# Stacking K's rows for two batches at once, with the weight check's squares moved between score groups

## The reference

```
q = layernorm(x) @ Wq.T + bq;  k = ctx @ Wk.T + bk;  v = ctx @ Wv.T + bv
scores = q k^T / sqrt(16) / temperature[head];  attn = softmax(scores)
x = x + (attn v) @ Wo.T + bo
gate = layernorm(x) @ Wg.T;  up = layernorm(x) @ Wu.T      # integer weights x 1/127, 768 wide
x = x + (silu(gate) * up) @ Wd.T                            # Wd likewise
```

## Time and profile before

| | |
|---|---|
| time, median of 3 runs | 410.93 us (410.18 to 411.25) |
| the profiled execution | 409.33 us, span 407.6 us |
| mean granted TensorE clock | 0.975 of full speed |
| busy: PE / DVE / ACT / Pool | 363.9 / 298.2 / 256.2 / 158.7 us |
| all DMA traffic | 37.68 MB, mean 92 GB/s |
| Q rows: DMAs, size, median from issue to landing | 96, 128.0 KB, 4.5 us |
| K rows: the same | 96, 60.0 KB, 2.6 us |

### The profile page before, as it was taken

How to read it: one execution, slowest core, us unless ns; L and a number is a source line. 1 busy time by engine, 2 the same in 40 slices (tenths; PEclk the granted TensorE clock), 3 DMA queues, 4 the chain that set the end, 5 groups by cost and what they waited for, 6 DMA issues and landing times.

```text
span 407.6 us, 9738 instructions
## 1 busy us (share of the span) xinstructions
PE 363.9 (89%) x3398; PEld 326.9 (80%) x3398; DVE 298.2 (73%) x734; ACT 256.2 (63%) x564; POOL 158.7 (39%) x282
## 2 busy tenths in 40 slices
PE   0567578799999999999999999999998999998984
PEld 0566465688999899989999898999997988787984
DVE  6974657678878877787788778888777686745743
ACT  2353366577776767676777686767766675756442
POOL 3133313264434443343426263626353061613322
PEclk9979689999999999999999999999999999999989
DMA  6999595536523753184525591739137622010000
GB/s 174 294 101 155 76 157 88 87 76 123 101 65 77 141 118 78 33 161 110 112 58 89 124 157 32 141 53 159 26 84 83 113 31 81 15 42 2 27 27 27
DMA packets 61749, 37.68 MB, mean 92 GB/s; under 512 B 34049, under 2 KB 61185, under 8 KB 61697
## 3 DMA queue, kind: packets, MB, share of 16 engines
q1 hardware_dynamic: 61696, 36.99, 47.4%
...
## 4 chain that ended last, share of the span: by engine, by line
PE 67%; DMA 11%; SPq 6%; DVE 5%; ACT 4%; issue 3%; POOL 3%; ACTq 0%; DVEq 0%
PE ps_w L807 28%; DMA qs<-q 9%; PE ps_w L800 9%; PE ps_o L936 6%; PE ps_b L920 6%; PE ps_a L910 6%; SPq L395 5%; PE ps_w L792 5%; PE ps_w L819 4%; PE ps_w L840 3%; DMA ks<-k 1%; ACT probs L545 1%; DVE ks L695 1%; POOL hidT L463 1%; DMA probs<-wkT 1%
## 5 line engine op out<-in xcount | busy, mean ns | idle before, releaser
L463 POOL TENSOR_TENSOR hidT<-hid,hidT 128x256 fp32r<-128x256 f32 x80 | 58.9, 738 | 124.7 <-ACT hidT L538 124.7
L807 PE MATMUL ps_w<-xn2T,wg 128*128 128x256 f32 x384 | 103.0, 301 | 0.2 <-DVE xn2T L632 0.2
L807 PE MATMUL ps_w<-xn2T,wu 128*128 128x256 f32 x384 | 96.2, 282 | 0.0
L545 ACT ACTIVATE probs<-ps_b 120x512 f32<-120x512 f32 x128 | 76.0, 593 | 22.8 <-PE ps_b L920 22.5
L710 DVE TENSOR_REDUCE negmax<-ps_a 128x4 f32<-128x480 f32 x128 | 82.8, 648 | 8.7 <-PE ps_a L910 8.4
L807 PEld LDWEIGHTS ps_w<-xn2T,wg 128*128 128x128 f32 x384 | 72.9, 190 | 1.5 <-issue 0.5
L807 PEld LDWEIGHTS ps_w<-xn2T,wu 128*128 128x128 f32 x384 | 73.1, 190 | 0.0
L910 PE MATMUL ps_a<-ks,qs 96*128 96x120 bf16 x512 | 49.9, 222 | 12.0 <-DMA qs<-q 7.5
L556 ACT ACTIVATE tanh_g<-ps_w 128x256 f32<-128x256 f32 x96 | 36.8, 383 | 37.2 <-PE ps_w L807 35.9
L807 PE MATMUL ps_w<-wd,hidT 128*128 128x256 f32 x384 | 55.8, 293 | 3.0 <-POOL hidT L463 2.6
L920 PE MATMUL ps_b<-qs,ks 98*120 98x256 bf16 x256 | 50.6, 279 | 4.6 <-ACT probs L545 3.2
...
## 6 DMA issues: line engine op xcount, KB each, us to landing
qs<-q SPq DMA_DIRECT2D x96, 128.0 KB, 4.5
ks<-k SPq DMA_DIRECT2D x96, 60.0 KB, 2.6
...
```

Of the source, the lines that this page charges most:

```text
L463: nc.gpsimd.tensor_tensor(hidT[:, 1, f], hid[:, f % 2], hidT[:, 0, f].bitcast(F32), ALU.subtract).then_inc(hid_lo, 1)
L545: nc.scalar.activation(probs[0:NKV, e % PROBS], ps_b[0:NKV], ACT.Exp).then_inc(exp_done, 1)
L807: last = nc.tensor.matmul(dst, lhsT, rhs, start=(start and k == 0), stop=(stop and k == len(terms) - 1), skip_group_check=True)
```

## The change

1. `ks` becomes two buffers, each for a pair of batches side by side ([98, 16 heads, 2, 120]) in place of three for one batch. In even batches the six K DMAs carry both batches; in odd ones none is issued. A and B read their half. The counts of the semaphore `ks_in` follow pairs (`pair_count`).
2. The ones rows are set by two memsets on Pool, at its start, in place of three on DVE.
3. K's hi part waits for one pair instead of for two batches.
4. The six pieces of squares go from steps -20 to -9 to steps -10 to 12, between A groups of batch 0; tell, sum, told and read go later as well.
5. Nearly all entries of the tables that are for the first four and last three batches, and some lags (k third, q third, rsqrt1, ctx hi, k mid, hid lo, y, store, load x_res), take other values.

The tables, `SHIFT` cut to the kinds that the text speaks of, and the code:

```diff
 LAG = {
-    "load ctx": -90, "load x": -90, "ctx lo": -77, "rsqrt1": -75, "ctx hi": -70, "stats1": -70, "var1": -66,
-    "norm1": -55, "k hi": -52, "normT1 hi": -51, "k rest": -50, "normT1 lo": -49, "k rows": -46, "k mid": -43,
-    "q hi": -40, "q rows": -37, "k third": -37, "q rest": -37, "v": -35, "q mid": -33, "q third": -31,
-    "A": -16, "max": -13, "load x_res": 6, "shift rows": 14, "shift hi": 16, "shift lo": 19, "exp": 27,
+    "load ctx": -90, "load x": -90, "ctx lo": -77, "stats1": -70, "rsqrt1": -69, "ctx hi": -69, "var1": -66,
+    "norm1": -55, "k hi": -52, "normT1 hi": -51, "k rest": -50, "normT1 lo": -49, "k rows": -46, "k mid": -44,
+    "q hi": -40, "q rows": -37, "q rest": -37, "v": -35, "k third": -33, "q third": -33, "q mid": -33,
+    "A": -16, "max": -13, "load x_res": 7, "shift rows": 14, "shift hi": 16, "shift lo": 19, "exp": 27,
     "B": 27, "bias x_res": 30, "pv": 40, "pv copy": 43, "rsum": 63, "att": 64, "attT hi": 69,
     "attT lo": 70, "rsqrt2": 77, "x1": 78, "stats2": 79, "var2": 80, "norm2": 89, "normT2 hi": 89,
-    "normT2 lo": 91, "tanh": 94, "gate": 95, "hid": 96, "hid hi": 98, "hid lo": 100, "hid lo last": 118,
-    "y": 123, "store": 148,
+    "normT2 lo": 91, "tanh": 94, "gate": 95, "hid": 96, "hid hi": 98, "hid lo": 99, "hid lo last": 118,
+    "y": 122, "store": 146,
 }
 EVERY = {
     "rsum": 1, "k rows": 4, "q rows": 2, "exp": 4, "A": 4, "B": 4, "max": 4, "pv": 16, "pv copy": 15,
-    "tanh": 4, "gate": 4, "hid": 4, "hid hi": 4, "hid lo": 2, "y": 4,
+    "tanh": 4, "gate": 4, "hid": 4, "hid hi": 4, "hid lo": 2, "y": 5,
 }
 
 
 START = {
-    "load wv": -96, "load wo": -44, "load bv": -116, "load bo": -21, "weight q": -72, "weight o": -25,
-    "weight v": -51, "ones rows": -133, "load wg": (-57, -51), "load wu": (-47, -45), "load wd": (-42, -40), "int hi": (-46, -29, -21),
-    "int lo": (-36, -25, -18), "squares": (-20, -19, -15, -14, -11, -9), "tell": -3, "sum": 2, "told": 7, "read": 63,
+    "load wv": -96, "load wo": -47, "load bv": -124, "load bo": 10, "weight q": -74, "weight o": -35,
+    "weight v": -54, "load wg": (-57, -51), "load wu": (-51, -45), "load wd": (-42, -40), "int hi": (-46, -29, -22), "int lo": (-36, -25, -18),
+    "squares": (-10, -6, -2, 2, 6, 12), "tell": 14, "sum": 20, "told": 18, "read": 78,
 }
 
 
 SHIFT = {
-    "A": {0: 5, 1: 2, 3: -1, 14: -1, 15: -1},
+    "A": {0: 3, 1: 1, 2: -1, 3: -1, 13: -1, 15: -1},
+    "B": {1: -4},
...
-    "bias x_res": {0: -16, 1: 9, 2: 4, 3: -16, 13: 10, 14: 8, 15: -5},
-    "ctx lo": {0: -66, 1: -29, 2: -6, 3: 7, 14: -4, 15: -8},
-    "k hi": {0: -20, 1: 19, 2: 2, 15: -6},
-    "k rest": {0: -21, 1: -27, 2: -12, 3: -27, 13: 4, 15: -1},
-    "k rows": {0: 4, 1: -9, 15: 3},
-    "k third": {1: 6, 2: 4, 3: 4, 14: 3, 15: -4},
-    "load x": {0: -49, 2: -19, 3: -23, 13: -5, 14: -27, 15: -12},
-    "load x_res": {0: -1, 3: -1, 14: 22, 15: -9},
-    "max": {0: 1, 2: -1, 14: -2, 15: -2},
-    "q rows": {0: -3, 1: 5, 2: 6, 3: 5, 14: 1, 15: -1},
-    "q third": {2: 3, 3: 1, 15: 4},
-    "rsqrt1": {0: -71, 3: -3, 14: -6, 15: -3},
+    "bias x_res": {0: -17, 1: 23, 2: 4, 3: -16, 14: 6, 15: -9},
+    "ctx lo": {0: -22, 1: -27, 2: -5, 3: -14, 13: 6, 14: -6, 15: 8},
+    "k hi": {0: -23, 1: 14, 2: 3, 3: -2, 15: -14},
+    "k rest": {0: -19, 1: -35, 2: -12, 13: 4, 15: -2},
+    "k rows": {0: 4, 13: -20, 14: -2, 15: 5},
+    "k third": {0: 3, 1: 12, 2: -12, 3: 12, 13: -5},
+    "load x": {0: -12, 1: -4, 2: -1, 13: -6, 14: -18, 15: 7},
+    "load x_res": {0: 4, 2: -1, 3: -14, 13: -4, 14: -1, 15: -1},
+    "max": {0: -1, 2: -1, 13: -2, 15: -2},
+    "q rows": {0: -3, 1: 9, 2: 6, 3: 5, 13: 5, 14: 2, 15: -7},
+    "q third": {0: -1, 1: 3, 2: 5, 3: -5, 13: -3, 14: 4, 15: -5},
+    "rsqrt1": {0: -75, 1: -9, 2: 2, 3: -3, 13: -3, 14: -9, 15: -2},
-    "stats1": {0: -88, 1: -48, 2: -8, 3: -10, 13: -2, 14: -2, 15: -1},
+    "stats1": {0: -75, 1: -55, 2: -2, 3: -6, 13: -4, 14: -2, 15: -1},
-    "var1": {0: -73, 1: -11, 2: -5, 3: -9, 13: -3, 14: 1, 15: 1},
+    "var1": {0: -74, 1: -9, 2: -2, 3: -10, 14: -6},
...
+
+
+def pair_count(pair):
+
+    return (pair // 2 + 1) * (6 * 16)
 
 
@@ -253,7 +260,7 @@
 
 
         qs = [sb(f"qs{r}", [KS_ROWS + 2, H, NQ], BF16) for r in range(RING)]
-        ks = [sb(f"ks{r}", [KS_ROWS + 2, H, NKV], BF16) for r in range(RING)]
+        ks = [sb(f"ks{r}", [KS_ROWS + 2, H, 2, NKV], BF16) for r in range(2)]
         v_one = [sb(f"v_one{r}", [NKV, H, VW]) for r in range(RING)]
         negmax = sb("negmax", [P, RING, QT, H])
         shiftT = sb("shiftT", [H, 2, NQ], BF16)
@@ -286,7 +293,7 @@
         xres_in = [sem(f"xres_in{r}") for r in range(RING)]
         ctx_in = [sem(f"ctx_in{r}") for r in range(2)]
         qs_in = [sem(f"qs_in{r}") for r in range(RING)]
-        ks_in = [sem(f"ks_in{r}") for r in range(RING)]
+        ks_in = [sem(f"ks_in{r}") for r in range(2)]
         shift_in = [sem(f"shift_in{r}") for r in range(RING)]
         stored = [sem(f"stored{r}") for r in range(RING)]
 
@@ -385,14 +392,17 @@
             sp.dma_start(bq_col[:], bq).then_inc(temp_in, 16)
             load_weight("q", wqT)
 
-            def stack(kind, n, part, t, dst, arrived, parts):
+            def stack(kind, n, part):
 
                 at_least(sp, b_full, count(n - RING, GROUPS, GROUPS))
                 sp.wait_ge((hi, mid, lowest)[part][kind], job_count(kind, 0, n))
-                src = t[:, part, :, n % 2] if kind == "k" else t[:, part]
+                if kind == "k":
+                    dst, src, arrived, parts = ks[n // 2 % 2], k3[:, part], ks_in[n // 2 % 2], K_PARTS
+                else:
+                    dst, src, arrived, parts = qs[n % RING], q3[:, part], qs_in[n % RING], Q_PARTS
                 for r in range(len(parts)):
                     if parts[r] == part:
-                        sp.dma_start(dst[n % RING][r * D:(r + 1) * D], src).then_inc(arrived[n % RING], 16)
+                        sp.dma_start(dst[r * D:(r + 1) * D], src).then_inc(arrived, 16)
 
             def step(i):
                 if i == START["load wv"]:
@@ -417,14 +427,15 @@
                     for part in range(2):
                         sp.dma_start(qs[n % RING][KS_ROWS + part:KS_ROWS + part + 1], shiftT[:, part]).then_inc(shift_in[n % RING], 16)
                 for n, part in due("k rows", i, 3):
-                    stack("k", n, part, k3, ks, ks_in, K_PARTS)
+                    if n % 2 == 0:
+                        stack("k", n, part)
                 for n, _ in due("load x_res", i):
                     at_least(sp, emptied["wo"], count(n - RING, 1, 1))
                     if n == 0:
                         sp.wait_ge(gint_lo, 3)
                     sp.dma_start(x_res[:, n % RING], x[n].rearrange("(t p) c -> p t c", p=P)).then_inc(xres_in[n % RING], 16)
                 for n, part in due("q rows", i, 3):
-                    stack("q", n, part, q3, qs, qs_in, Q_PARTS)
+                    stack("q", n, part)
                 for n, _ in due("store", i):
                     sp.wait_ge(emptied["down"], count(n, QT, QT))
                     sp.dma_start(out[n].rearrange("(t p) c -> p t c", p=P), y[:, n % RING]).then_inc(stored[n % RING], 16)
@@ -446,6 +457,9 @@
             nc.gpsimd.memset(zero_col[:], 0.0)
             nc.gpsimd.memset(ones_col[:], 1.0).then_inc(consts_done, 1)
             pool.wait_ge(consts_done, 1)
+            for pair in range(2):
+                nc.gpsimd.memset(ks[pair][KS_ROWS:], 1.0).then_inc(k_ones_set, 1)
+                pool.wait_ge(k_ones_set, pair + 1)
 
             def rsqrt(which, n, got, eps_sem, out_sem, norm_sem):
 
@@ -506,11 +520,12 @@
                 act.wait_ge(full[kind], count(n, 1, 1))
                 nc.scalar.activation(dst, src, ACT.Copy).then_inc(hi[kind], 1)
 
-            def highest(kind, n, t, w, bias, arrived):
-
-                for back in ((2, 1) if kind == "k" else (1,)):
-                    if n >= back:
-                        act.wait_ge(arrived[(n - back) % RING], slot_count(n - back, 1, 1) * (6 * 16))
+            def highest(kind, n, t, w, bias):
+
+                if kind == "k" and n > 0:
+                    act.wait_ge(ks_in[(n // 2 - 1) % 2], pair_count(n // 2 - 1))
+                if kind == "q" and n > 0:
+                    act.wait_ge(qs_in[(n - 1) % RING], slot_count(n - 1, 1, 1) * (6 * 16))
                 if kind == "k" and n == 0:
                     act.wait_ge(bk_in, 16)
                 act.wait_ge(full[kind], job_count(kind, 0, n))
@@ -545,7 +560,7 @@
                     nc.scalar.activation(probs[0:NKV, e % PROBS], ps_b[0:NKV], ACT.Exp).then_inc(exp_done, 1)
                 for n, _ in due("k hi", i):
                     if n % 2 == 0:
-                        highest("k", n, k3.rearrange("p a c b k -> p a c (b k)"), 2 * NKV, bk_col, ks_in)
+                        highest("k", n, k3.rearrange("p a c b k -> p a c (b k)"), 2 * NKV, bk_col)
                 for n, half in due("pv copy", i, 2):
```

(14 more changed lines are left out.)

46 lines of the change are left out of this document (21 added, 25 removed), and 39 rows, old and new, of the table SHIFT.

## The result

The changed kernel takes **416.71 us** (median of 4 runs, 414.75 to 418.42); the kernel before took 410.56 beside it (4 runs). The ratio is 1.016, 95% interval 1.0117 to 1.0203: slower by 1.6%, which a measurement here can tell from no change. The forecast was 415.1, range 407.5 to 418.0. The profiled execution took 415.63 us with a span of 413.5.

A forecast was written before the change was run, and what follows sets the result against it. Latency and transfers bound the first some 80 us, then PE, waiting for Q's rows at even batches. Steady part +7.6 us and front -3.4 gave +4.2 on the median of 410.93: 415.1 us, range 407.5 to 418.0.

The forecast's parts named there:

- the swap on Pool: Even batches 6 to 14: k third falls behind the bias on Pool, putting 1.4 us into the chain to Q's landing.
- K's bytes, 0.3 each: Even batches: K's doubled DMA just ahead of Q delays Q's start by up to 0.5 us, taken as 0.3.
- rival 1: Even batches: Q's landing not tied to k third, slack of SP and rings absorbs 1.43 us; 407 us, chance 0.23.
- Batch 12: Waits for nothing before; loses var1's shift at batch 13 and becomes like batch 10, waiting 2.0 us: +2.0.
- Batch 14: Same swap adds 1.7 us, but PE's group moves behind a gate-up job of 1.42 us: +0.2.
- The front: First some 80 us, made by latency and transfers: three effects sum to -3.4 us, from 0 to -6.
- (a): Start: DVE loses three memsets, Q's first rows leave at 19.3 not 21.34, first group near 31.5 instead of 33.39.
- (b): Front: squares move at no cost, K's next hi part waits less; batch 2's first group gains 1.7 us.
- (c): Batch 3 has no K transfer left; PE's wait of 1.55 us at 76.78 goes, gaining no more than 1.7.
- The squares: Front: 36 matmuls move between batch 0's groups into PE's idle time, costing nothing; without that cover 4.3 us.
- rival 3: Start: Pool's memsets take 6 us each, batch 0's rsqrt at 13.6 instead of 6.64; 420 us, chance 0.08.
- rival 2: Transfers go by pieces, not bytes: even batches cost 5.7, front gains 3 more; 410.2 us, chance 0.15.

The follow-up runs named there:

- K's third first: Kernel before with K's third part moved ahead of the next batch's rsqrt on Pool in even batches 4 to 14: 406.49 us, ratio 0.9907.
- the memsets behind the third parts: Changed kernel with K's third part ahead of the rsqrt, and Pool's two memsets moved behind batch 0's third parts of K and Q: 407.17 us, ratio 0.9925.

## Why the prediction was right, and where its steps failed

The direction was right, and so was the main step, the swap on Pool. The sum was near (+4.2 against +5.9 in the traces and +6.2 in the medians), but in part by luck: four misses of 1.5 to 2.8 us went in both directions. Point by point, from the starts of the first score groups:

| step | forecast | measured |
|---|---|---|
| up to batch 4's first group | -3.1 | -0.3 |
| batches 6, 8 and 10 | +5.1 | +3.6 |
| batch 12 | +2.0 | +2.1 |
| batch 14, to batch 15's first group | +0.2 | +1.9 |
| from there to the end | 0 | -1.5 |

- **The swap on Pool** is what makes the kernel slower. It is shown both ways: taken out of the changed kernel it gives back all 7.1 us; put into the kernel before it costs 10. The period of two batches from 6 to 14 is 44.7 us, forecast 44.5, and 42.8 without the waits.
- **Its size** at batches 6, 8 and 10 was forecast as 1.7 a batch. The added wait was 1.0, 1.2 and 0.9 us, so that at 6 and 10 PE waits 1.1 and 1.2 us and not the forecast's near 2. The term "K's bytes, 0.3 each" is zero: without the swap the waits are as before with K doubled, and half the bytes shorten none of them. And of the bias's 1.43 us some 0.3 come back: at batch 10 SP issues Q's six in 3.81 us, against 4.45 with the swap undone, and from the first issue to the landing 8.4 us pass and not 8.7. That was the slack of rival 1, there but small. (The forecast's bounds of 5.7 and 8.5 for this part add up, from its own terms, to 5.8 and 8.8; nothing hangs on it.)
- **Batch 12** was right in size, and the traces have the chain that was forecast: in the changed kernel its third ends 10.2 us ahead of the first group (9.5 at batch 10), and no longer 12.1. That the shift of var1 is what was lost there is argued from the tables.
- **Batch 14** was right in its own step and lacked another. PE's group moved behind a gate-up job, as forecast, and more of PE's order changed around it: from 13 to 14 the changed order needs 21.7 us where the old one needs 19.2, and gets back 1.1 from 12 to 13 and 0.7 from 14 to 15 (read from kernels whose score groups wait for nothing there). What that costs with the waits is seen from batch 12's first group to batch 15's: 63.4 us in the kernel before, 63.8 in the changed kernel with early squares, whose wait of 2.2 us is the same as the changed kernel's. That is +0.4, forecast +0.2. The changed kernel itself took 65.4, because of what no step had: PE's clock fell behind the wait of 2.2 us (stretches of the changed kernel, columns as above):

```profile
318.00:322.00 4.00, 2.65 (x23) 2.64 (x24) 1.93 (x5) 1.43 (x3) 1.92 (x5) 0.87 0.58 125
322.00:326.00 4.00, 4.00 (x36) 3.28 (x34) 1.90 (x5) 2.30 (x5) 0.00 (x0) 0.71 0.13 33
```

  From 14 to 15 this execution needs 20.3 us; the six others with this order of work, none with such a fall there, need 18.7 to 19.3.
- **The front** was mis-sized by nearly 3 us. (a) The direction held: Q's first rows left at 20.48 (forecast 19.3), 0.9 earlier than before, and the first group gained as much; in three others with this start they left at 19.26, 19.27 and 20.49. From there to the last landing it took 11.8 us, forecast 12.4. (b) "Batch 2 gains 1.7" failed: +0.1. The step had Q's first issue of batch 2 come 2.5 us earlier; it came 0.75 earlier (49.94, 50.69). It cannot leave before ACT has ended Q's hi part, at 49.28 (50.52 before), which starts as soon as PE's product for Q is there, and now K's last three issues stand ahead of it until 49.9; the step saw only the K transfers. The last of the six then landed 6.2 us after its issue and not 5.4: K's doubled rows cost 1.0 us at batch 2, where the forecast allowed 0.8, and 1.0 at batch 4, where it had 0.3. (c) Batch 3's wait is gone, as forecast, and its group came 1.5 us closer to batch 2's.
- **The squares** cost nothing in the time, as forecast, but not for the reason given. They don't all lie in idle time in either place: in the kernel before a piece of 0.78 us stood right ahead of the first group, and moved late, in the kernel before with K's third first, they put batch 2's group 1.3 us later. The piece also costs more than estimated: six matmuls took 0.86 us at the full clock and 1.52 at 1.2 GHz, 6.5 us for the six pieces in the changed kernel, not 4.3.
- **Pool's memsets** took 3.3 us each, as taken from DVE's row, so rival 3 fell. Batch 0's rsqrt started at 8.56, forecast 8.3. But "a delay that lies inside (a)" was wrong for K: behind that rsqrt Pool makes the low part of the context, K's matmuls wait for it until 11.26 (10.06 before), and K's first rows left 1.2 us later than before (15.09, 13.89). With the memsets moved away they left at 13.15. The memsets hold DVE's cast of wk as well, which is the chain only where it comes late, as in the trace with half of K's bytes.

The start of the changed kernel, Pool, SP and PE in turn (PE's first line is K's product, the other the first score group):

```profile
1.67 6.81 POOL L461 MEMSET ks<- 2x3840 bf16 x2
8.56 0.20 POOL L467 TENSOR_TENSOR minus_mean<-zero_col,meanvar 128x2 f32<-128x2 f32 x1
...
9.92 1.20 POOL L497 TENSOR_TENSOR ctxT<-ctx_raw,ctxT 128x480 fp32r<-128x480 f32 x1
```

```profile
15.09 1.99 SPq L405 DMA_DIRECT2D ks<-k  x3
...
20.48 1.84 SPq L405 DMA_DIRECT2D qs<-q  x3
```

```profile
11.26 2.89 PE L803 MATMUL ps_w<-ctxT,wk 128*128 128x240 f32 x12 [11.26 <-POOL ctxT L497]
...
32.45 0.37 PE L921 MATMUL ps_a<-ks,qs 96*128 96x120 bf16 x4 [2.36 <-DMA ks<-k]
```

  The first group now waits 2.4 us for K's last row (landed at 32.3, Q's last at 31.5); the forecast counted both transfers in one sum.
- **The piece counts** of the prediction were wrong: K's pieces go from 240 to 960 bytes, and the packets fall from 61,749 to 42,547; they are not the same in both kernels. So rival 2 rested on more than I gave it. It fell all the same: at batches 2 and 4 half the bytes, in smaller pieces and twice as many, took the wait away. The Trainium skill's line that pieces under 512 bytes miss the line rate (DMA: Bandwidth & Descriptors, Specifications) thus brought this kernel nothing that a wait shows. The prediction also read it too widely: the same page, under Why small descriptors are slow (HBM only), says that transfers from SBUF to SBUF, which K's are, do not suffer from small pieces. The traces agree: in the kernel before, K's DMAs of 60 KB in 240-byte pieces landed 0.5 to 0.6 us apart where they came closest (at the 116 GB/s of Q's rows a DMA of this size would take 0.53).
- **The end** comes 1.5 us closer behind batch 15's group, which the prediction counted at 0. In the kernel before, PE ran at 0.78 and 0.79 of the clock from 388 to 396 us, in the changed kernel from 380 to 400 at the full clock. The distance from batch 15's group to the end lies between 73.8 and 75.4 us in all profiled executions of this study. It is shortest, 73.8 and 73.9, in the two traces (the changed kernel and the one with the memsets behind the third parts) in which PE's clock holds from batch 15 to the last 0.4 us, so the 1.5 us look like the clock, by chance, and not like the tables. It was not tried by itself.

**What stays open:** the parts of the 10 us of the swap alone (6.9 of waits, 4.4 behind three falls of the clock, 2.2 in the front) are read from one trace, 3 us slower than the median; how often the falls come in other executions was not measured, nor why the waits grew there by up to 1.9 us for a bias of 1.43. Why so little of the earlier start reaches batch 2 is read off two traces only. Nor is it known why the kernel with the memsets behind the third parts varies by 4 us.
